# Adding the classes' running counts inside the rank product: an accumulated f32 product on TensorE in place of VectorE's addition

## The reference

```python
def reference(x, ...):
    x = x + conv_attention(layernorm(x))
    t = x.reshape(8, 1024, 64)
    xf = layernorm(t).reshape(-1, 64)
    gate_logits = xf @ Wg + bg
    top_w, top_i = jax.lax.top_k(gate_logits, 2)
    top_w = jax.nn.softmax(top_w, axis=-1)
    w_dense = jnp.sum(jax.nn.one_hot(top_i, 8) * top_w[..., None], axis=1)
    for e in range(8):
        h = jax.nn.gelu(xf @ W1[e] + b1[e], approximate=False)
        out = out + w_dense[:, e:e + 1] * (h @ W2[e] + b2[e])
    return t + out
```

## Time and profile before

| | |
|---|---|
| median of 3 runs | 451.93 us (451.66 to 452.38) |
| the profiled execution's own time | 450.36 us |
| its span | 448.6 us |
| its mean granted TensorE clock | 0.974 of full speed |

### The profile page before, as it was taken

The page is one execution under the profiler, slowest core; times in us unless marked ns, Lnnn a source line. Parts: engine busy times, 40 slices in busy tenths (PEclk is TensorE's granted clock), DMA queues, the critical chain, the costliest instruction groups (busy, mean ns, idle before and its releaser), DMA issues. The chain is left out here.

```text
span 448.6 us, 12510 instructions
## 1 busy us (share of the span) xinstructions
PE 409.8 (91%) x3921; PEld 277.0 (62%) x3921; DVE 351.9 (78%) x1240; ACT 334.9 (75%) x889; POOL 304.3 (68%) x406
## 2 busy tenths in 40 slices
PE   6897989899999899899899789698999999999995
PEld 5354434445454444445445345245999999999995
DVE  4688979977888978868969989888876688778532
ACT  2466688788877787777787665444988898888884
POOL 4233434775855889888888858466777777777765
PEclk8899989999999999989999899989999999999998
DMA  9916800000000000000000000014332222222310
GB/s 221 233 48 124 183 2 2 1 1 1 2 1 2 14 20 20 21 18 14 20 21 14 24 26 32 19 49 105 99 75 76 64 58 59 62 71 73 78 45 0
DMA packets 36168, 22.42 MB, mean 50 GB/s; under 512 B 13648, under 2 KB 33855, under 8 KB 36104
## 3 DMA queue, kind: packets, MB, share of 16 engines
q1 hardware_dynamic: 30264, 14.70, 14.7%
q0 software_dynamic: 4960, 6.45, 4.4%
q10 hardware_dynamic: 880, 0.48, 0.7%
HBM read 13.07 MB, written 9.27 MB: 50 GB/s over the span
## 5 line engine op out<-in xcount | busy, mean ns | idle before, releaser
L672 POOL TENSOR_TENSOR pn<-pe_,rs 128x512 f32<-128x512 f32 x64 | 67.2, 1050 | 65.4 <-DVE rs L1213 61.3
L1509 PE MATMUL bank<-aa,bd 64*64 64x256 f32 x512 | 70.5, 392 | 12.2 <-ACT pt L821 8.7
L642 POOL DMA_INDIRECT rows_hbm<-rowb,posu x64 | 65.7, 1026 | 23.2 <-issue 17.2
L687 POOL DMA_INDIRECT out<-bt,zs x63 | 62.8, 996 | 21.5 <-issue 16.1
L1512 PE MATMUL bank<-pt,bt 64*64 64x256 f32 x512 | 70.5, 393 | 0.0
L1202 DVE TENSOR_REDUCE mx<-bank 128x8 f32<-128x512 f32 x64 | 43.8, 684 | 31.4 <-PE bank L1509 31.0
L833 ACT ACTIVATE pe_<-sc 128x512 f32<-128x512 f32 x64 | 40.6, 635 | 33.2 <-DVE sc L1205 23.0
L1509 PEld LDWEIGHTS bank<-aa,bd 64*64 64x64 f32 x512 | 33.5, 133 | 46.0 <-issue 35.7
L793 ACT COPY zs<-bank 128x512 f32<-128x512 f32 x64 | 37.2, 581 | 15.0 <-PE bank L1512 14.9
L1205 DVE TENSOR_TENSOR sc<-bank,mx 128x512 f32<-128x512 f32 x64 | 44.2, 691 | 2.2
L1325 DVE SCALAR_TENSOR_TENSOR bt<-bank,zs 128x64 f32<-128x64 f32 x91 | 25.4, 280 | 25.6 <-PE bank L1692 24.3
(11 more groups left out here) (298 smaller groups left out, 1042.0 us busy)
## 6 DMA issues: line engine op xcount, KB each, us to landing
zs<-rows_hbm SPq DMA_DIRECT2D x91, 66.0 KB, 2.2
wloc<-in_L_conv_w_local SPq DMA_DIRECT2D x2, 1152.0 KB, 8.8
rows_hbm<-zrow SPq DMA_DIRECT2D x1, 1914.0 KB, 13.6
x_sb<-in_x SPq DMA_DIRECT2D x3, 512.0 KB, 10.9
wloc<-in_L_ffn_W SPq DMA_DIRECT2D x2, 512.0 KB, 6.8
rows_hbm<-rowb,posu POOLq DMA_INDIRECT x64
out<-bt,zs POOLq DMA_INDIRECT x63, 2.3
wrec<-in_w2b SPq DMA_DIRECT2D x1, 520.0 KB, 4.3
```

What stands on the lines that cost most here:

```text
L642: nc.gpsimd.indirect_dma_start(out=rows_hbm, out_offset=bass.IndirectOffsetOnAxis(ap=posu[:, t:t + 1], axis=0), in_=rowb[:, t], in_offset= ...
L672: nc.gpsimd.tensor_tensor(pn[:, v % 2, :].rearrange("p (h j) -> p h j", h=HEADS), pe_[:, v % 2], rs[:, v % 2].unsqueeze(2).broadcast_to([P ...
L687: nc.gpsimd.indirect_dma_start(out=out, out_offset=bass.IndirectOffsetOnAxis(ap=idx_j, axis=0), in_=ob[:, j % LANES], in_offset=None, boun ...
L1509: scored = nc.tensor.matmul(dots[v % 2][same, w * 2 * P:(w + 1) * 2 * P], xq[same, t % 2, 2 * v + w], aa[same, t % 2, :, j0:j0 + WT], star ...
```

## The change

TensorE opens each batch's accumulation with one more product: a row of 128 ones (`ones32[0:1]`, f32) by one row of 28 counts, repeated nine times (252 columns, f32). The counts are those of `cst_sb` for b = 0, and after that the ninth slot of `rk` that the batch before left there. So `rk` already holds what the addition gave, and its ninth slot the counts after the batch. VectorE's addition, its count upkeep (b = 4 to 7) and the first copy of the counts, GpSimd's upkeep (b = 0 to 3), the tile `cnt` and the two semaphores of it go away. To have room for the wider `ones32`, `bt` is laid out densely, at half its size: its rows of 64 used values no longer stand 128 apart.

```diff
-              ..., weights=17, place=17, counts=18,
+              ..., weights=17, place=17,
...
-        ones32 = sb("ones32", [P, CLS])
+        ones32 = sb("ones32", [P, P])
...
-        bt = sb("bt", [P, 2, TG * 2, P])
+        bt = sb("bt", [P, 2, TG * 2, C])
...
-        cnt = sb("cnt", [P, CLS])
...
-        xw = bt[:, :, :, 0:C]
+        xw = bt[:]
...
-            def counts(b):
-
-                n = TG * BATCH[b][1]
-                wait(pool, counts_used, b + 1)
-                wait(pool, counts_ready, b)
-                nc.gpsimd.tensor_tensor(cnt[:], cnt[:], rk[:, n], ALU.add).then_inc(counts_ready, 1)
...
                 wait(act, rank_done, b + 1)
                 wait(act, pos_ready, b)
-                wait(act, counts_ready, min(b, ASIDE))
                 nc.scalar.copy(rk[:, 0:n + 1], ...).then_inc(rank_ready, 1)
...
                 wait(dve, rank_ready, b + 1)
-                if b == 0:
-                    rstep(nc.vector.tensor_copy(cnt[:], cst_sb[:, 1]))
                 dve.wait_ge(route_step, rn[0])
-                wait(dve, counts_ready, min(b, ASIDE))
-                added = nc.vector.tensor_tensor(pr_[:, 0:n], rk[:, 0:n], cnt[:].unsqueeze(1).broadcast_to([P, n, CLS]), ALU.add)
-                if b < ASIDE:
-                    added.then_inc(counts_used, 1)
-                    wait(dve, counts_used, b + 1)
-                else:
-                    rlink(added)
-                    rstep(nc.vector.tensor_tensor(cnt[:], cnt[:], rk[:, n], ALU.add))
-                rlink(nc.vector.tensor_tensor(pr_[:, 0:n], pr_[:, 0:n], oh[:, 0:n], ALU.mult))
+                counted[0] = n
+                rlink(nc.vector.tensor_tensor(pr_[:, 0:n], rk[:, 0:n], oh[:, 0:n], ALU.mult))
...
-                nc.vector.scalar_tensor_tensor(lastu[:], cnt[0:1], float(-P), base[0:1], ALU.add, ALU.max)
+                nc.vector.scalar_tensor_tensor(lastu[:], rk[0:1, counted[0]], float(-P), base[0:1], ALU.add, ALU.max)
...
                 out_ = rank_words(b)
                 src = oh[:].rearrange("p t k -> p (t k)")
-                nc.tensor.matmul(out_, seq16[:, 0], src[:, 0:(n + 1) * CLS], start=True, stop=False)
+                counted = cst_sb[0:1, 1] if b == 0 else rk[0:1, TG * BATCH[b - 1][1]]
+                nc.tensor.matmul(out_.rearrange("p (t k) -> p t k", k=CLS), ones32[0:1, :], counted.unsqueeze(1).broadcast_to([1, n + 1, CLS]),
+                                 start=True, stop=False)
+                nc.tensor.matmul(out_, seq16[:, 0], src[:, 0:(n + 1) * CLS], start=False, stop=False)
```

More of the change, by code:

```diff
@@ L111 @@
 STEADY = dict(norm=(1, 2, 3), halves=(4, 5, 6, 7), low=(6, 8), turned=9, xs=10, gate=11, gate_out=11, logits=11, top=(12, 12),
-              index=(13, 13), classes=(13, 14), gaps=14, tanh=16, ranks=15, ranks_out=15, weights=17, place=17, counts=18,
+              index=(13, 13), classes=(13, 14), gaps=14, tanh=16, ranks=15, ranks_out=15, weights=17, place=17,
               send=(18, 19, 20, 21, 22, 23, 24, 25))
@@ L370, in program @@
         pairs_ready = sem("pairs_ready")
-        counts_used = sem("counts_used")
-        counts_ready = sem("counts_ready")
         tanh_ready = sem("tanh_ready")
@@ L659, in body @@
                             gaps(b)
-                    for b, k in due("counts", g, u):
-                        if b < ASIDE:
-                            counts(b)
                     for b, k in due("send", g, u):
@@ L1028, in weights @@
                 nc.vector.tensor_scalar(rowb[:, tiles, 2 * C + 1], th[:, 0:n], -0.5, 0.5, ALU.mult, ALU.add).then_inc(weights_ready, 1)
+            counted = [0]
             def positions(b):
@@ L1097, in last_blocks @@
                 dve.wait_ge(route_step, rn[0])
-                nc.vector.scalar_tensor_tensor(lastu[:], cnt[0:1], float(-P), base[0:1], ALU.add, ALU.max).then_inc(last_ready, 1)
+                nc.vector.scalar_tensor_tensor(lastu[:], rk[0:1, counted[0]], float(-P), base[0:1], ALU.add, ALU.max).then_inc(last_ready, 1)
             def full_blocks(part):
@@ L1110, in count_full @@
                 rstep(nc.vector.tensor_copy(tbl[:, 0:2], cst_sb[:, 2:4]))
-                rlink(nc.vector.tensor_tensor(tbl[:, 3], cnt[:], base, ALU.subtract))
+                rlink(nc.vector.tensor_tensor(tbl[:, 3], rk[:, counted[0]], base, ALU.subtract))
                 rlink(nc.vector.tensor_scalar(tblu[:, 0], tbl[:, 3], float(P - 1), float(P), ALU.add, ALU.max))
@@ L1121, in scan_full @@
             def scan_full(f):
-                rlink(nc.vector.tensor_tensor_scan(tbl[:, 4], ones32[:], f, 0.0, ALU.mult, ALU.add))
+                rlink(nc.vector.tensor_tensor_scan(tbl[:, 4], ones32[:, 0:CLS], f, 0.0, ALU.mult, ALU.add))
                 rlink(nc.vector.tensor_scalar(tbl[:, 5], tbl[:, 4], jcol, None, ALU.is_le))
```

## The result

The changed kernel took 456.25 us (median of 4 runs, 455.73 to 458.16), the kernel before in the same comparison 452.15 us (4 runs, 451.66 to 453.48): a ratio of 1.0116, 95% interval 1.008 to 1.0151. (A ratio here is the comparison's own, formed from the runs within 1.5% of a kernel's fastest, while medians, spreads and counts are of all runs.) The profiled execution took 455.73 us with a span of 453.9. The forecast of 452.3 us, no difference that can be told, was wrong. The kernel is slower by about 1%.

What follows compares the result with a forecast made beforehand. TensorE and ScalarE were taken to form one line at the ranks, on the chain for b = 4, 5, 7. 2.10 - 0.84 - 0.92 = +0.3 us on the median 451.93 gave 452.3 us, range 450.9 to 454.3.

Steps and rivals of the forecast that it cites:

- the first term: TensorE ahead of each batch's rank products: one added f32 product costs 0.42 us, counted in five batches, +2.10 us.
- rival 1: b = 1 and 3: slack fails, product paid every loop batch; 453.5 to 453.9 us, 455.1 at 0.70 each; chance 0.36.
- Where it counts: The product's 0.42 us counts in b = 0, 2, 4, 5 and 7, and is hidden in b = 1, 3 and 6.
- the slack argument: b = 1 and 3: GpSimd's pn starts 0.55 us after the needed reciprocal is done, so the product's 0.42 us is hidden.
- the multiplication would stand in the addition's wait: VectorE, b = 3: the multiplication moves up, waits for GpSimd and ends where the addition did; 0.42 us goes, not 1.2.
- rival 2: Positions on VectorE, b = 0, 2, 3: the multiplication escapes the wait for GpSimd; 1.7 us better, 450.6 us; chance 0.14.
- The removed step of 0.42 us in b = 3: VectorE's positions: the step from multiplication to reduction goes, counted in b = 0 and b = 3, together -0.84 us.
- ScalarE's copy stood idle: ScalarE's rank copy: a sign of being right was idle time of about 1.0 instead of 0.55 us.
- GpSimd, -0.92 us: GpSimd ahead of the first send in b = 0 to 3: four count additions removed, 0.23 us each, -0.92 us.
- The 0.52 us of idle before the send stay: GpSimd ahead of the first send of b = 3: its idle time of 0.52 us would remain.
- The removals together: Work taken off VectorE (-0.84 us) and GpSimd (-0.92 us), together 1.76 us.
- The clock: TensorE at 188 to 192 us: a shift spares or adds one 1.2 us low-clock stretch, 451.1 or 453.5; chance 0.03 for one more.

Runs made afterwards that it cites:

- rows128: Changed kernel with the counts' product given 128 rows, ones in row 0 and zeros below in the stationary operand: 449.16 us, ratio 0.9982 to the kernel before.
- layout: Kernel before with only the change's layout, bt dense and ones32 128 wide: 449.92 us, ratio 1.0005 to the kernel before.
- zero128: Kernel before with the new layout plus a 128-row f32 product of zeros a batch, counts still added on VectorE: 452.58 us, ratio 1.0066.
- zero_product: Kernel before with the new layout plus a one-row f32 product of zeros a batch, counts still on VectorE and GpSimd: 456.78 us, ratio 1.014.
- after_again: The changed kernel once more, nothing else altered, against the kernel before: 457.13 us, ratio 1.0154.
- last1: Changed kernel with 128-row products for b = 0 to 6 and the one-row product for b = 7 alone: 453.99 us, ratio 1.0062.

## Why the prediction was wrong, step by step

**The step that failed** is the first term, the price of the product: "I take 0.42, since operand type and columns are those of the first row and the weight load has work ahead of it to hide behind". The row was right for what it showed, neighbours of one shape. A product with one row among products with 128 has its weight load late on the way in and the next one late on the way out, and measured 0.71 us: the upper end that the text had given, 0.70. The sum's rule for it would have been rival 1, and its condition, a delay over 0.55 us in b = 1 and 3, held: GpSimd idle 0.25 us for the reciprocal in both, and in b = 2 as well. (Its figure at 0.70 was 455.1 us, the nearest of the text to the 456.25 measured, though part of the latter is the clock.) At 0.42 it does not hold: in `rows128`, with 0.47, `pn` has no idle time at either place, and the whole change came out at 0.9982. GpSimd's timeline of `rows128`, b = 1 and b = 3:

```profile
172.77 1.04 POOL L663 TENSOR_TENSOR pn<-pe_,rs 128x512 f32<-128x512 f32 x1
...
235.83 1.04 POOL L663 TENSOR_TENSOR pn<-pe_,rs 128x512 f32<-128x512 f32 x1
```

**Where it counts: b = 2 was misread.** The 128-row product with the counts kept passes on 0.48 us from b = 0, nothing from b = 1 and 2, and 0.1 from b = 3: 0.56 us, where the forecast had 0.84 for b = 0 and 2. I had counted b = 2 for an idle time of 0.97 us at 205.89; but in that execution the clock had fallen at 188 us, shortly ahead of it. In `layout`, where it had not, VectorE and GpSimd in b = 2 look as in b = 1 and 3, with 0.55 us of slack and no idle time:

```profile
205.73 0.20 DVE L1213 RECIPROCAL rs<-sm 128x8 f32<-128x8 f32 x1
...
206.48 1.03 POOL L672 TENSOR_TENSOR pn<-pe_,rs 128x512 f32<-128x512 f32 x1
```

The one-row product passes on 0.74 us from b = 0 and 0.26, 0.25 and 0.37 from the others, 1.62 in all. That is one in full and three over their slack, by which 0.71 + 3 x (0.71 - 0.55) = 1.19; the idle time of 0.25 us says that 0.46 rather than 0.55 us was hidden. So the slack argument stood, at the right price. From b = 4 on the product cost 1.86 us with 128 rows and 1.68 with one, where three products would be 1.26 at 0.42 and 2.13 at 0.71; as the clock lost more with the 128 rows (5.0 against 3.4 us), these two do not set a price.

**VectorE.** That the multiplication would stand in the addition's wait was right; rival 2 is out. The removed step of 0.42 us in b = 3 is seen (`pn` idle 1.03 instead of 1.45 us), but the maximum behind it comes no earlier for it: `rows128` is 0.96 us ahead of `zero128` at the copy of b = 3 and 0.96 at that maximum. ScalarE's copy stood idle 1.27 us (forecast 1.0; 1.02 in `rows128`).

**GpSimd, -0.92 us.** At the sends themselves less came back. For b = 3 the send starts 0.62 us behind L588's end (249.07 to 249.69); before, 0.72 us behind the same instruction's end (246.70 to 247.42). That is 0.10 us, the same in b = 1 and 2; in b = 0 it is nothing. "The 0.52 us of idle before the send stay" was wrong; what the send waits for beside the addition is not shown.

**The removals together.** Forecast 1.76 us, all but b = 3's 0.23 on GpSimd in the first part of the table. Measured there, `zero128` less `rows128` gives 0.96 us: 0.47 for b = 0 (forecast 0.65), 0.24 and 0.26 for b = 1 and 2 (0.23 each), nothing for b = 3 (0.42). `zero_product` less `after_again` gives 0.77: 0.19, 0.30, 0.27 and nothing. Behind it the 128-row pair, whose clocks lost the same, gives 1.61 us. There VectorE lost an addition and the counts' upkeep in every batch, and I had priced both at nothing beside a busy TensorE. That these two brought it was not tried one by one, and the one-row pair, with 0.67 us, lost 3.4 and 1.7 us to the clock and can't confirm it. Nor do the medians agree on a worth: `zero_product`, expected up to 1.8 us above the changed kernel, is 0.35 us below `after_again`, and `zero128` is 3.8 us above `rows128` by the ratios (0.0084). The forecast sum for a product of 0.42 us, +0.3, stands beside the -0.15 that `rows128` measured.

**The clock** was given a chance of 0.03. Of the 7.15 us by which `after_again` is slower it has some 5, by the filler. In the first comparison's 4.1 us it has another part. The profiled execution there, with 5.3 us more span than that of before, has no fall at the expert stage: 3.05 us came ahead of the routing, which `after_again` does not repeat, and 2.69 in b = 4 to 7, of which 1.36 are gone in `after_again`, with one stretch at the lower level less; the two other parts are 0.14 and 0.30 us shorter. The rival looked at the right kind of place, TensorE idle for ScalarE, and at the wrong one: not the loop at 188 us, but the wait of 0.46 and 1.38 us around the table load, with 140 us of unbroken work behind it. The prediction had treated an added stretch as a 1.2 us affair; here it lasted up to 13.7 us and cost up to 6.5 (`last1`).

**What stays open** is why an added product makes this fall frequent. The gap is as long before as after (0.46 and 1.38 us in both), the kernel before kept its clock there in its profiled execution, some long runs have no low clock to show, and even `rows128` and `zero128`, whose products are no dearer than any other, had long runs in a third of the cases. Filler at other places, or a table load moved away from there, was not tried.

## What to carry to other kernels

A small product between large ones is priced with its surroundings: give it the neighbours' number of rows, zeros in the added ones, and read the gap between weight loads, not the duration of the product. Slack covers a delay only up to its own size, so a term that rests on slack needs the price's upper end, too; here 0.55 us lay between 0.42 and 0.71. A slack or an idle time read from one execution is worth a look at the clock just ahead of it: b = 2's 0.97 us was the clock's doing. And ahead of a long stage without pauses, where some executions lose their clock, it is worth trying to fill a wait of TensorE of a microsecond or two with products that nobody reads: six of them took 5 us off the changed kernel's median, and nothing that can be told off a kernel without the added product.

## What the runs showed of the hardware

- A change between 128 rows and 1 or 32 rows cost 0.24 us for the way in and back (0.94 against 0.70 us from the product ahead to the f16 one, with one or 32 rows against 128), once for two products in a row. The weight load of the 64-row scores behind 128-row products had no idle time ahead of it.
- An f32 weight load with few rows is no shorter: the new one with one row took 182 ns at the median, those with 128 rows 189 ns in `rows128`.
- A granted clock of 0.50 behind idle times of 0.46 and 1.38 us lasted 13.6 us of unbroken work in `zero_product`; the kernel before, with the same idle times, kept 1.00 there.
